# Attention in 48 steps: one score tile and one row maximum per step, projections in pieces, two work banks, heads in two buffers

## The reference, cut to what matters

```python
# 8 sequences of 384 tokens, 512 wide: 256 rows of a state-space kernel, 128 rows of text
x = layernorm(concat(h, txt))
q, k, v = x @ Wq.T, x @ Wk.T, x @ Wv.T          # 16 heads and 4 key/value heads of 32
q, k = rope(q), rope(k)
attn = softmax(q @ k.T * 32 ** -0.5)            # each key/value head serves 4 heads
h2 = residual + (attn @ v) @ Wo.T
x2 = layernorm(h2)                              # routing: softmax, top 6 of 64 experts,
out = h2 + experts(x2) + shared_expert(x2)      # a slot of 64 per expert
```

## Time and profile before

| what | value |
|---|---|
| median of 3 runs | 1734.31 us (1725.32 to 1750.95) |
| the profiled execution | 1740.46 us |
| its span, first to last instruction | 1738.8 us |
| mean granted TensorE clock | 0.817 of full |
| TensorE busy | 1422.9 us, 82% |
| VectorE, ScalarE, GpSimd busy | 758.3, 390.8, 423.7 us |

### The profile page before, as it was taken

One profiled execution on the slowest core, in us unless ns is written; L12 is line 12 of the kernel. 1 busy time (PEld: TensorE's weight loads), 2 busy tenths in 40 slices (PEclk: granted clock), 3 DMA queues, 4 the chain that ended last, 5 costly groups with the idle time before them and its releaser, 6 DMA issues. The chain is left out here.

```text
span 1738.8 us, 23830 instructions
## 1 busy us (share of the span) xinstructions
PE 1422.9 (82%) x9120; PEld 895.6 (52%) x9120; DVE 758.3 (44%) x1633; ACT 390.8 (22%) x636; POOL 423.7 (24%) x455
## 2 busy tenths in 40 slices
PE   3195788888888888888888762199999999999995
PEld 2194453545436354363543431166666666666663
DVE  7982645455545555455454441322323223222221
ACT  2121122323233232332332411211111112111110
POOL 3000110100332323322233246312222222222221
PEclk7597676878859678596685885599999999999998
DMA  2023211323212232122221251597979889898882
GB/s 95 0 64 83 54 34 35 71 53 89 73 47 66 51 90 73 43 68 53 71 74 36 75 175 40 138 341 249 332 248 323 270 262 332 246 324 274 281 244 34
DMA packets 129837, 239.54 MB, mean 138 GB/s; under 512 B 58056, under 2 KB 64088, under 8 KB 129752
## 3 DMA queue, kind: packets, MB, share of 16 engines
q1 hardware_dynamic: 114232, 214.16, 39.4%
q0 software_dynamic: 15520, 24.22, 6.9%
HBM read 175.66 MB, written 38.90 MB: 123 GB/s over the span
## 5 line engine op out<-in xcount | busy, mean ns | idle before, releaser
L949 DVE TENSOR_REDUCE at_maxes<-at_ps 128x1 f32<-128x384 f32 x384 | 196.7, 553 | 172.9 <-PE at_ps L663 171.7
L807 ACT ACTIVATE bulk<-at_ps 128x1152 f32<-128x1152 f32 x128 | 144.7, 1130 | 406.6 <-PE at_ps L633 406.2
L1311 PE MATMUL mo_ps<-mo_x2s,mo_sgu 128*117 128x384 f32 (+1 forms) x1152 | 221.1, 344 | 0.0
L663 PE MATMUL at_ps<-at_qhi 32*128 32x384 f32 x384 | 158.9, 623 | 64.8 <-DVE at_maxes L949 53.4
L1311 PEld LDWEIGHTS mo_ps<-mo_x2s,mo_sgu 128*117 128x117 f32 (+1 forms) x1152 | 198.8, 181 | 13.7 <-issue 13.5
L1532 POOL DMA_INDIRECT out_rows<-mo_y,mo_scatter_ix x64 | 92.1, 1439 | 401.2 <-DMA out_rows<-mo_y,mo_scatter_ix 214.9
L663 PEld LDWEIGHTS at_ps<-at_qhi 32*128 32x128 f32 x384 | 72.0, 258 | 188.2 <-DVE at_maxes L949 153.6
L1112 POOL DMA_INDIRECT slot_table<-at_toki,at_si x144 | 141.1, 980 | 51.0 <-issue 48.3
L623 PE MATMUL at_ps<-WxT,at_xT 128*128 128x512 f32 (+1 forms) x576 | 119.9, 364 | 17.4 <-ACT at_v L852 15.6
L633 PE MATMUL at_ps<-at_QT 97*128 97x384 f32 x384 | 123.3, 439 | 6.9 <-ACT bulk L807 6.9
L1074 POOL TENSOR_TENSOR at_oTs<-at_oT,at_oTs 128x384 fp32r<-128x384 f32 x32 | 32.0, 999 | 379.5 <-ACT at_oTs L819 379.5
(11 more groups left out here) (197 smaller groups left out, 1721.0 us busy)
## 6 DMA issues: line engine op xcount, KB each, us to landing
mo_wgu<-in_L_ffn_w_gate SPq DMA_DIRECT2D x32, 704.0 KB, 6.7
mo_wgu<-in_L_ffn_w_up SPq DMA_DIRECT2D x32, 704.0 KB, 8.3
bulk<-in_L_ffn_w_gate SPq DMA_DIRECT2D x32, 704.0 KB, 7.3
bulk<-in_L_ffn_w_up SPq DMA_DIRECT2D x32, 704.0 KB, 8.5
mo_wd<-in_L_ffn_w_down SPq DMA_DIRECT2D x32, 512.0 KB, 7.2
bulk<-in_L_ffn_w_down SPq DMA_DIRECT2D x32, 512.0 KB, 5.4
at_QT<-at_qhi SPq DMA_DIRECT2D x64, 192.0 KB
rows_scores<-at_x SPq DMA_DIRECT2D x8, 864.0 KB, 3.7
```

The lines of the kernel that those rows point to most:

```text
L663: T.matmul(ps[:, 5 + u % 2, 0:SEQ], qhi[rows, r, s * P:(s + 1) * P], qhi[rows, REP, :], start=True, stop=True).then_inc(raw_scores, 1)
L807: A.activation(PT[:, N % RING, :, :], ps[:, 0:NT, 0:SEQ], ACT.Exp, scale=float(HD) ** -0.5)\
L949: V.tensor_reduce(maxes[:, s, h:h + 1], ps[:, 5 + u % 2, 0:SEQ], AX.X, ALU.max, negate=True)\
L1311: m = M.matmul(ps[0:SW[c], 5 + g, 0:SEQ], sgu[:, wa, g, k, SO[c]:SO[c] + SW[c]], x2s[:, xa, k, :], start=(k3 == 0), stop=(k3 == 3 * KC - 1))
```

## The change

An iteration now has 48 steps `t`. Each step has at most one score matmul (one tile of keys of one head, two banks in turn) with an exponential of its own, and one raw score with its maximum. Raws run 15 steps ahead of the scores that need them (`LEAD`), in the order of the scores: 12 in a row for one key/value head g, all on the same 32 rows. Maxima are turned per group of 12 and stacked by a DMA of their own (6 KB). Projections come in pieces of one k (3 matmuls) or two (6 matmuls of 256 columns). Work banks are 6 and 7, raw scores use 4 and 5. `qhi` has two buffers, and `logits(c)` moves into the iteration before. GpSimd's indirect DMAs come one per step from step 30 on, with the second norm's deviation in step 37.

```diff
-        qhi = sb("at_qhi", [P, NTILE, SEQ], F32R)
+        qhi = sb("at_qhi", [P, 2, NTILE, SEQ], F32R)
...
-        mrow = sb("at_mrow", [NH // 2, 2, SEQ], F32R)
+        mrow = sb("at_mrow", [REP, 2, SEQ], F32R)
...
+        STEPS = NH * NT
+        GROUP = REP * NT
+        STACK = 16 * 6
+        LEAD = GROUP + 3
+        SCORE, O, SUMS, RAW, WORK = 0, 2, 3, 4, 6
+        TILES = (REP, 0, 1, 2, 3)
+        X_AT = {0: (0, 1), 1: (2, 3)}
+        Q_AT = {2 + 6 * s + k: (s, k) for s in range(NT) for k in range(KC)}
+        KV_AT = {6 + 6 * s + j: (s, (2 * j, 2 * j + 1)) for s in range(NT) for j in range(2)}
+        OUT_AT = {t0 + k: (s, k) for s, t0 in enumerate((20, 27, 31)) for k in range(KC)}
+        HEADS_AT = {24: (0, 1), 25: (2, 3), 26: (4,)}
+        X2_AT = {41: 0, 42: 1, 43: 2, 44: 3}
+        OUT_HI_AT = {0: -2, 12: -1, 36: 0, 38: 1}
+        VALUES_AT = {1: 0, 2: 1, 4: 2, 5: 3, 7: 4, 8: 5}
...
+            def stack_max(a, g):
+                sp.wait_ge(mrow_ready, NKV * a + g + 1)
+                wait(sp, scores_ready, STEPS * (a - 1) + GROUP * (g + 1))
+                sp.dma_start(QT[SPLIT:QR, REP * g:REP * (g + 1), :].bitcast(F32), mrow[:, g % 2, :].bitcast(F32))\
+                    .then_inc(max_stacked[g], 16)
...
+            def score(b, t):
+                h, kt = t // NT, t % NT
+                if t % GROUP == 0:
+                    pe.wait_ge(stacked[t // GROUP], STACK * (b + 1))
+                    pe.wait_ge(max_stacked[t // GROUP], 16 * (b + 1))
+                wait(pe, probs_ready, STEPS * b + t - 1)
+                T.matmul(ps[:, SCORE + t % 2, 0:SEQ], QT[:, NH + h // REP, kt * P:(kt + 1) * P], QT[:, h, :],
+                         start=True, stop=True).then_inc(scores_ready, 1)
...
+            def raw(a, g, j):
+
+                s, r = j % NT, j // NT
+                if j == 0 and g == 0:
                     pe.wait_ge(qhi_ready, NTILE * (a + 1))
...
+                if j == 1:
+                    wait(pe, mrow_ready, NKV * a + g)
+                wait(pe, max_ready, STEPS * a + GROUP * g + (j - 1 if j >= 2 else 0))
                 rows = slice(HD * g, HD * (g + 1))
...
+                for t in range(STEPS):
                     if main:
...
+                        score(b, t)
+                    if raw_at(b, t):
+                        raw(*raw_at(b, t))
+                    if turn_at(b, t):
+                        turn_maxes(*turn_at(b, t))
+                    if nxt:
+                        for k in X_AT.get(t, ()):
+                            turn_x(a, k)
+                        if t in Q_AT:
+                            project_q(a, *Q_AT[t])
+                        if t in KV_AT:
+                            project_kv(a, *KV_AT[t])
+                    if prev2 and t == 22:
                         places(d)
...
+                    if prev and t in OUT_AT:
+                        project_out(c, *OUT_AT[t])
+                    if nxt:
+                        for i in HEADS_AT.get(t, ()):
+                            turn_heads(a, i)
+                    if prev and t in X2_AT:
+                        turn_x2(c, X2_AT[t])
+                    if prev and t == 46:
+                        logits(c)
+                    if t % GROUP in VALUES_AT:
+                        values(NKV * b + t // GROUP - 1, VALUES_AT[t % GROUP])
...
+                for t in range(STEPS):
                     if main:
...
+                        exponential(b, t)
+                    if turn_at(b, t - 1):
+                        max_row(*turn_at(b, t - 1))
...
+                for t in range(STEPS):
+                    if raw_at(b, t):
+                        row_maximum(*raw_at(b, t))
+                    if t % GROUP == 9:
+                        divide(NKV * b + t // GROUP - 1)
+                    if nxt and t in (1, 2):
+                        x_lo(a, 2 * t - 2)
+                        x_lo(a, 2 * t - 1)
...
+                    if nxt:
+                        for i in HEADS_AT.get(t - 1, ()):
                             q_lo(a, i)
```

More of the change, by code:

```diff
@@ L502, in attention_phase @@
         heads_turned, qhi_ready, qlo_ready = sem("heads_turned"), sem("qhi_ready"), sem("qlo_ready")
-        stacked = [sem(f"stacked{i}") for i in range(2)]
+        stacked = [sem(f"stacked{g}") for g in range(NKV)]
+        max_stacked = [sem(f"max_stacked{g}") for g in range(NKV)]
         raw_scores, max_ready = sem("raw_scores"), sem("max_ready")
@@ L551, in rows_in, with stack @@
                 sp.dma_start(dst[:, S0 // P:NT, :], txt[b].rearrange("(s p) d -> p s d", p=P)).then_inc(done, 16)
[L553 to L566, removed]
+            def stack(a, g):
+                rows = slice(HD * g, HD * (g + 1))
+                heads = slice(REP * g, REP * (g + 1))
+                hi, lo = qhi[rows, a % 2], qlo[rows]
+                for n, part in enumerate((hi, lo, hi)):
+                    sp.dma_start(QT[HD * n:HD * (n + 1), heads, :].bitcast(F32), part[:, 0:REP, :].bitcast(F32))\
+                        .then_inc(stacked[g], 16)
+                for n, part in enumerate((hi, hi, lo)):
+                    sp.dma_start(QT[HD * n:HD * (n + 1), NH + g, :].bitcast(F32), part[:, REP, :].bitcast(F32))\
+                        .then_inc(stacked[g], 16)
+            def stack_max(a, g):
[3 more added lines that the diff above has]
+                    .then_inc(max_stacked[g], 16)
             rows_in(xn, 0, a_in)
@@ L572, in _ @@
                 if main:
[L574 to L577, removed]
+                    wait(sp, scores_ready, STEPS * b)
+                    stack(b, 3)
                 if nxt and a + 1 < B:
@@ L595, in _ @@
                     sp.wait_ge(qlo_ready, NTILE * (a + 1))
-                    wait(sp, scores_ready, NH * b + NH // 2)
-                    stack(0)
+                    for g in range(2):
+                        wait(sp, scores_ready, STEPS * b + GROUP * (g + 1))
+                        stack(a, g)
+                if main:
+                    stack_max(b, 3)
+                if nxt:
+                    wait(sp, scores_ready, STEPS * b + GROUP * 3)
+                    stack(a, 2)
                 if prev:
@@ L616, in _, with product @@
             pe.wait_ge(ones_ok, 1)
[L618 to L625, removed]
-                return m
-            def scores(b, h):
-                if h in (0, NH // 2):
-                    pe.wait_ge(stacked[2 * h // NH], STACK * (b + 1))
-                wait(pe, probs_ready, NH * b + h)
-                for kt in range(NT):
-                    m = T.matmul(ps[:, kt, 0:SEQ], QT[:, NH + h // REP, kt * P:(kt + 1) * P], QT[:, h, :],
-                                 start=True, stop=True)
-                m.then_inc(scores_ready, 1)
+            def product(out, xs, x_cols, ws, w_cols, k):
+                for n, (xa, wa) in enumerate(((0, 0), (0, 1), (1, 0))):
+                    m = T.matmul(out, xs[:, xa, k, x_cols], ws[:, wa, k, w_cols], start=(k == 0 and n == 0),
+                                 stop=(k == KC - 1 and n == 2))
+                return m
+            def score(b, t):
[6 more added lines that the diff above has]
+                         start=True, stop=True).then_inc(scores_ready, 1)
             def values(G, q):
@@ L675, in turn_x @@
                     pe.wait_ge(xn_ready, NT * (a + 1))
-                    wait(pe, mrow_ready, 2 * a)
-                    wait(pe, max_ready, UNITS * a)
+                    wait(pe, lg_copied, a - 2)
+                if k == 1:
+                    wait(pe, x2T_ready, KC * (a - 2))
                 if k >= 2:
```

347 lines of the change are left out of this document (147 added, 200 removed).

## The result

The changed kernel takes 2039.81 us (median of 4, 2031.4 to 2049.77) beside 1737.67 us before (4 runs): ratio 1.174, 95% interval 1.163 to 1.185. It is slower, as forecast, but by 302 us where the forecast said 151: inside the range over all rivals, 1680 to 2060, and outside the forecast's own, 1830 to 1960. The profiled execution took 2031.4 us, span 2029.7, 290.9 more than before. From first to last score attention takes 1300.34 - 206.45 = 1093.9 us against 1007.66 - 226.48 = 781.2: +312.7. The prologue gives back 20.0 us and the tail 1.8.

What follows compares the result with a forecast made beforehand. TensorE bounds attention, 56% of a steady period at low clock. Steady periods +84, others +27, +24, +19, +19, prologue -17, tail -5 sum to +151 us: 1885 us; own range 1830 to 1960, over rivals 1680 to 2060.

Steps and rivals of the forecast that it cites:

- prologue: Before attention: 15 raws instead of 48 put the first score at about 209 us, -17 us.
- tail: At the end: GpSimd issues seven of 18 scatters before the second norm's deviation, -5 us.
- A lone raw: In attention's steps: each of 48 raws stands alone, costing 0.38 us at full clock or 0.61 at half.
- waits for the max row: Each group's second raw waits for ScalarE's copy of the previous group's maxima, 1.1 us four times, 4.4 us per period.
- wait for low parts: Turned x tiles and heads wait for VectorE's low part, made behind the row maximum: five places, 8 us per period.
- The period's formula: Steady attention period is 1 / ((1 - s)/103 + s/166) us, 103 at full clock and 166 at half.
- share s: Share of an attention period that TensorE spends at half clock; bounds 0 and 1, break-even at 15%.
- I take s as it is now in each period, the nearest row there is: 0.56: Half-clock share kept from the kernel before: steady attention period 130 us, +21 for each of four, 84.
- 14 us of waits: TensorE's new waits per attention period: max row 4.4, low parts 8, second norm 1.5; 14 us at full clock.
- B: Rival: the even stream keeps attention's clock full, steady periods of 103 us, 1703 us in all; chance 0.27.
- 18 us row: Profile row of attention before: 18 us of scores, raws, values and transposes at 0.50 clock with TensorE always busy.
- C: Rival: attention's clock stays low throughout, steady periods of 166 us, +445 us, 2180 us in all; chance 0.13.

Runs made afterwards that it cites:

- a_waits: Changed kernel with the max-row copy moved ahead of the exponential and low parts ahead of the row maximum: 1795.00 us, ratio 1.023.
- a_noraw: Changed kernel without raw scores and row maxima (maxima 0, exponential's scale 1e-6): 1519.93 us.
- experiment 2: Raw scores and row maxima removed from both kernels: 1519.93 us for the changed kernel, 1495.37 us for the kernel before.
- experiment 3: Four separate edits of the changed kernel: scores and raws in twos 1.018, both waits moved 1.023, unread matmul per raw 1.117, 128-row raws 0.970.
- experiment 4: Changed kernel with only max-row copy moved 1.106, only low parts 1.056, both plus scores and raws in twos 0.971, both plus filler 1.014.
- b_alt: Kernel before with scores and raws alternating one by one in seven slots per period: 1782.63 us beside 1725.78.
- a_fill1: Changed kernel with one unread 128-row matmul of 384 columns ahead of every raw score: 1954.65 us, ratio 1.117.
- a_waits_fill1: Changed kernel with both waits moved away and an unread 128-row matmul ahead of every raw score: 1759.64 us, ratio 1.014.
- a_raw128: Changed kernel with each raw score computed from 128 constant rows instead of 32, giving wrong maxima: 1696.95 us, ratio 0.970.
- a_pw_fill1: Changed kernel with scores and raws in twos, both waits moved, unread matmul ahead of every second raw: 1834.93 us, ratio 1.047.

## Why the prediction was right and wrong

**Right:** the direction, and most prices of an instruction. A lone raw, and a score behind values or another raw, cost 0.37 to 0.38 us at full and 0.61 to 0.62 at half clock. The second raw of a group waits for the max row: 3.8 us per period where 4.4 were forecast. Turned tiles and one projection wait for low parts, 1.1 to 1.2 us each in four places, 4.5 us, where five of 1.6 were put. First score at 206.45 (209), prologue -20 (-17), tail -2 (-5). The period's formula holds too: with the measured share s = 0.86 it gives 1 / (0.14/103 + 0.86/166) = 152.9 us, and 153.6 was measured. That it fits so closely is in part luck, since two prices were off in opposite ways. The score behind a projection piece, about a third of all, costs 0.45 us at half clock and not 0.62; a piece between raw and values costs 936.74 - 935.17 = 1.57 us and not 1.41.

**Wrong:** the size came out at twice the forecast because of one step, "I take s as it is now in each period, the nearest row there is: 0.56". Measured was 0.86 in two steady periods and some 0.7 to 0.8 in the later ones (periods of 145.5, 139.2 and 147.1 us). With 0.56 a period is 130 us, so of the 44 us that such a period gained, 21 are the new order's own cost and the other 23 the clock's. The others came to 121 us for the first (forecast 112), 135 for the second (118), 154 for the third (126) and 100 for the last (77), all at a higher share than forecast. In the first the share was 0.92, with which its formula gives 134 us, so there the forecast's own prices were 13 us too high and hid part of the miss.

What fails in that step is that it took the share for a property of the stream, to be carried over, when the change alters it. It was also priced apart from the waits: 14 us of waits were a term in the sum and not a cause of the share. a_waits shows that they are both, since 7.8 us of idle time less took 41 us off. The outer range was drawn to a share of 0.8, which is why it held.

**The rivals.** B, full clock throughout, fell as the forecast's 18 us row had said: no period of after has more than 0.68. C, half throughout, was nearer in its share (0.86 against 1) than the forecast (0.56), but too slow by 140 us in sum, since stretches such as 694 to 703 still ran at full clock. The Trainium skill ("TensorE: Matmul & The Clock Gate", Part 1) ties the low clock to idleness. The runs agree in part: most falls that were read come at pauses, and fewer waits lift the grant. They differ in that 15 and 20 us without any idle stayed at 0.50, that a_waits fell behind 10 us with TensorE busy in 9.93, and that a_noraw idles 8.8 us of 76.9 at 0.93.

**What is shown, and what stays open.** Shown: the raws carry the cost (experiment 2), and in the new order the loss of clock needs both a raw of 32 rows standing alone and the new pauses; with either removed the grant is above that of the kernel before (experiment 3), with both removed the kernel is the fastest of the complete ones (experiment 4). Pauses alone don't settle when the clock falls: the falls that were read stand behind pauses of 2.2, 1.65, 1.1 and 0.36 us, and one behind none. What sets after's steady period apart is how long half clock lasts once it is there, 31 and 102 us against 17 and 34 in a_waits. Open: why lone raws and pauses don't lower the grant in the old order (b_alt, 0.76); why steps of score, raw, projection and values hold half clock in after once it has fallen, where full-row matmuls in the same places (a_fill1, a_waits_fill1) bring it back, and why they don't in the order in twos. That the 32-row matmul counts for little in what the chip grants by would fit after, a_fill1 and a_raw128, but not a_pw_fill1; it is argued, not shown.

## What to carry to other kernels

When TensorE's grant is below 1 in a bound stage, price a new pause or a new neighbour twice, by its length and by what it does to the share at half clock, and let the range span that share; for the waits here the second was four times the first (33 us against 7.8). In an order written by hand, keep small-row matmuls next to each other, and let the engine that TensorE waits for do its small copy or low part ahead of its bulk work: these two edits turned +17% into -3%. A filler is a gamble: it moved the ratio by -0.057 in after and by +0.076 where it split pairs.

## What the runs showed that I had not expected

- Added work made the kernel faster: 48 unread matmuls per period took the ratio from 1.174 (after) to 1.117. On top of a_waits they did at least no harm (1.023 to 1.014, intervals overlapping). The same matmul ahead of each pair in the old order cost 4.5%.
- Two raws in a row on the same 32 rows take 0.54 us at full clock against 0.74 for two lone ones and 0.38 for two on two row groups. So more than half of what a pair saves is in entering and leaving, and the rest in two row groups at once.
- A filler behind a score was nearly free of entry costs: in a_waits_fill1 score, filler and raw take 0.28, 0.27 and 0.37 us at full clock, 0.92 in all, where score and raw alone take 0.75. It adds 0.17 us, about the time of its 384 columns. Between two raws (a_pw_fill1) the same matmul takes 0.37 us.

```profile
601.75 0.44 PE L654 MATMUL at_ps<-at_QT 97*128 97x384 f32 x1
602.03 0.34 PE L683 MATMUL at_ps<-WoT 128*128 128x384 f32 x1
602.30 0.43 PE L685 MATMUL at_ps<-at_qhi 32*128 32x384 f32 x1
602.67 0.97 PE L644 MATMUL at_ps<-WoT,at_oTs 128*128 128x512 f32 x3
```

- Half clock holds through 15 us of steps with projection and values and no gap (660 to 675 in after), while in the kernel before the stretches with projections ran at 1.00.
